# Tile 4's pair sums on GpSimd are held until tile 2's heads have been added on VectorE

## The reference, cut to what matters

```
x = x + L0_ffn(L0_cond(x, cond))          # attention, then product keys:
    sim = q . keys                        # per token, 8 heads, two halves of 32 keys
    all_scores = sx[..., :, None] + sy[..., None, :]
    scores, pk = top_k(all_scores, 8); h = gelu(x . down[idx])
    out = sum over heads and picks of softmax(scores) * h * up[idx]
x = x + L1_ffn(L1_cond(x, cond))          # 8 experts 128-256-256-128 (relu), top 2,
                                          # then 8 experts 128-512-128 (gelu), top 2
```

## Time and profile before

| | |
|---|---|
| median of 3 runs | 769.32 us (769.05 to 769.36) |
| the profiled execution | 770.8 us, of which 769.0 us span |
| PE busy | 730.4 us, 95% of the span |
| VectorE, ScalarE, GpSimd busy | 73%, 74%, 41% |
| mean granted TensorE clock | 0.991 of full |

### The profile page before, as it was taken

How to read it: one execution, slowest core, us unless ns; L and a number is a source line. 1 busy time by engine, 2 the same in 40 slices (tenths; PEclk the granted TensorE clock), 3 DMA queues, 4 the chain that set the end, 5 groups by cost and what they waited for, 6 DMA issues and landing times.

```text
span 769.0 us, 14737 instructions
## 1 busy us (share of the span) xinstructions
PE 730.4 (95%) x5250; PEld 644.6 (84%) x5250; DVE 560.2 (73%) x1495; ACT 572.4 (74%) x1001; POOL 312.3 (41%) x214
## 2 busy tenths in 40 slices
PE   6989998979768999999999999999999999999998
PEld 4767777879657898899899998988998999999887
DVE  3889997596699669777976897697779747834421
ACT  3788886299688789779868987897798689453243
POOL 2122221499993546175325635461753251000000
PEclk9999999989989999999999999999999999999999
DMA  8940000000000000000000000000000000000000
GB/s 312 339 128 2 3 1 2 1 1 1 1 0 1 1 2 7 1 2 7 1 3 0 9 1 2 1 8 0 2 8 0 2 1 8 1 1 9 1 1 7
DMA packets 11159, 16.91 MB, mean 22 GB/s; under 512 B 680, under 2 KB 6992, under 8 KB 10832
## 3 DMA queue, kind: packets, MB, share of 16 engines
q1 hardware_dynamic: 10944, 15.72, 6.3%
q10 hardware_dynamic: 144, 0.26, 0.1%
HBM read 14.93 MB, written 1.05 MB: 21 GB/s over the span
## 4 chain that ended last, share of the span: by engine, by line
PE 82%; DVE 8%; issue 5%; ACT 3%; DMA 1%; SPq 0%; DVEq 0%; ACTq 0%
PE banks L453 77%; PE banks L489 3%; DVE W_both L1223 2%; PE banks L703 2%; ACT G_both L947 2%; DVE W_both L1455 1%; DMA region<-in_pA 1%; ACT region L1024 1%; DVE acc L1601 1%; DVE HF L1461 0%; PE banks L735 0%; DVE region L1216 0%; ACT region L1030 0%; DVE PT L1553 0%; PE banks L796 0%
## 5 line engine op out<-in xcount | busy, mean ns | idle before, releaser
L395 POOL TENSOR_TENSOR region<-sim 128x1024 f32<-128x1024 f32 x128 | 261.6, 2072 | 95.8 <-DVE top_keys L1412 58.7
L1086 ACT ACTIVATE HF<-banks,lpack 128x256 f32<-128x256 f32 x256 | 105.4, 479 | 55.6 <-PE banks L453 54.6
L1024 ACT ACTIVATE region<-region,neg_thr 128x1024 f32<-128x1024 f32 x128 | 143.8, 1153 | 0.0
L1455 DVE SCALAR_TENSOR_TENSOR W_both<-region,rz_rel,W_both 128x1024 f32<-128x1024 f32 x98 | 139.9, 1428 | 2.0 <-DVE W_both L1455 0.5
L453 PE MATMUL banks<-HF,w_sb 128*128 128x256 f32 x512 | 123.2, 384 | 5.9 <-DVE HF L1461 5.8
L453 PEld LDWEIGHTS banks<-f_sb,HF 128*128 128x128 f32 x1024 | 123.7, 192 | 3.4
L1030 ACT ACTIVATE region<-region,dtop 128x1024 f32<-128x1024 f32 x114 | 125.4, 1142 | 0.0
L453 PE MATMUL banks<-f_sb,HF 128*128 128x128 f32 x1024 | 124.5, 275 | 0.0
L453 PE MATMUL banks<-cT,f_sb 128*128 128x256 f32 x512 | 122.7, 382 | 0.1
L453 PEld LDWEIGHTS banks<-HF,w_sb 128*128 128x128 f32 x512 | 94.6, 193 | 17.7 <-DVE HF L1461 6.7
L453 PEld LDWEIGHTS banks<-cT,f_sb 128*128 128x128 f32 x512 | 92.1, 190 | 16.3 <-issue 2.9
(11 more groups left out here) (167 smaller groups left out, 1011.5 us busy)
## 6 DMA issues: line engine op xcount, KB each, us to landing
w_sb<-in_w SPq DMA_DIRECT2D x1, 2048.0 KB, 12.8
f_sb<-in_f SPq DMA_DIRECT2D x1, 2048.0 KB, 15.5
region<-in_wq SPq DMA_DIRECT2D x1, 1024.0 KB, 8.6
region<-in_wqT SPq DMA_DIRECT2D x1, 1024.0 KB, 10.8
w_sb<-in_w SPq DMA_DIRECT2D x1, 1024.0 KB, 8.5
out_x<-acc_f SPq DMA_DIRECT2D x16, 64.0 KB, 1.6
x1T_all<-in_xT SPq DMA_DIRECT2D x1, 768.0 KB, 8.0
region<-in_pA SPq DMA_DIRECT2D x1, 588.5 KB, 6.5
```

The lines of the kernel that those rows point to most:

```text
L395: pool.tensor_tensor(S[a][h].rearrange("p (i j) -> p i j", i=NK), sim[t % 3][:, h, :].unsqueeze(2).broadcast_to([P, NK, NK]), sim[t % 3][: ...
L1024: act.activation(S[a][h], S[a][h], ACT.Prelu, bias=neg_thr[t % 4][:, h:h + 1], alpha=STEEP).then_inc(h_L, 1)
L1086: m = act.activation(HF[e % 2][:, f, :], bank(2 + b, 256 * (f % 2), 256 * (f % 2) + 256), ACT.Gelu_apprx_tanh, bias=L("bf", 4 * e + f, 4 * ...
L1455: v.scalar_tensor_tensor(W[a], S[a][h], rz_rel[a][:, h:h + 1], W[a], ALU.mult, ALU.add).then_inc(h_w, 1)
```

## The change

In turn 1, and only there, GpSimd waits ahead of tile 4's head 3 until h_w is 7, which is when all seven additions of tile 2 are done. Without it head h waits for h_w at h. Heads 4 to 7 stand behind head 3 in GpSimd's list and so are held as well, and so is the copy behind them. No instruction is added, removed or put in another place on any engine but the wait.

```
                 if more:
                     for h in range(8):
+                        if g == 1 and h == 3:
+                            pool.wait_ge(h_w, 7)
                         pair_scores(t + 2, 0, h)
                 keep_x2(t, 0)
```

## The result

Over six runs of each, the changed kernel takes 772.41 us (772.02 to 772.95) and the kernel before 769.54 (769.05 to 770.59): ratio 1.0034, 95% interval 1.0023 to 1.0045, 2.9 us slower. 772.2 had been predicted.

A forecast was written before the change was run, and what follows sets the result against it. VectorE was taken to bound turn 1 ahead of L796, and PE the stretch from there on. VectorE's net +1.24 us and the clock's 1.7 made +2.9, so 772.2 us, with an 8 in 10 range of 768.5 to 774.2.

The forecast's parts named there:

- What it takes away: VectorE from 225.2 us to tile 2's last addition runs undisturbed: 4.23 us saved, 3.08 left after waits for PE.
- What it adds: Tile 3's four additions on VectorE each meet one of GpSimd's held pair sums: 4.32 us of new loss.
- On PE: Small gaps in turn 1 gather into one of 3.7 us, from 245.65 to L796's start at 249.34.
- The net delay: VectorE's new loss less its saving, 4.32 - 3.08, delays the end by +1.24 us.
- The clock: PE's granted clock falls at the new gap; price 1.7 us, the middle between nothing and 3.4.
- The full loss of 2.8: By the skill's rule, each wait lowers PE's clock: 2.8 us on top of 1.24, in sum +4.0.
- The prediction's main ground for a clock that stays up: PE's clock stayed at 1.00 through the gap of 1.76 us ahead of turn 1.
- Clock up: Rival: PE's clock stays up behind the new gap, only +1.24 us remains, 770.6 us; chance 0.27.
- The third addition in between: Rival: tile 3's third addition on VectorE runs before the next pair sum, saving 1.87 us, 768.7 us; chance 0.11.
- The faster one: Rival: held sums cost VectorE nothing in tile 3; PE's three gaps, 2.69 us, are gained, 766.6 us; chance 0.10.

The follow-up runs named there:

- hold5: The changed kernel with the wait asking for h_w at 5 instead of 7; 769.97 us against 769.61 for the kernel before.
- hold9: The changed kernel with the wait asking for h_w at 9 instead of 7; 770.12 us against 769.61 for the kernel before.
- hold11: The changed kernel with the wait asking for h_w at 11 instead of 7; 770.88 us against 769.61 for the kernel before.
- fill: The changed kernel plus six unused 128x256 matmuls on PE in the gap ahead of L796; 770.73 us against 769.61 for the kernel before.
- hold11_fill: The changed kernel with the wait at 11 and five unused matmuls on PE ahead of the gate's matmuls; 769.79 us against 769.70 before.

## Why the prediction was right

**What it takes away: right.** L1447 fell to 0.23, the single addition to 1.28, the pair to 2.65. Tile 2's last addition ended at 233.54, 15.54 after the mark; 234.51 - 218.62 = 15.89 was predicted. The 0.35 is the wait for expert 6's values: 1.03 was forecast (230.07 - 229.07, the two times it comes from, is 1.00), 0.63 came. I had taken PE's group ahead of it from before with its 1.71 us; part of it ran at the lower clock, and this time it took 1.37, as the clock was back 10.4 us after the mark instead of 11.1. That is not the change: the clock's fall in the gap of 4.6 us, ahead of all that the change does, had come 0.7 us sooner too.

**What it adds: right.** From tile 2's last addition to the end of the eighth expert the prediction had 10.45 + 4.32 = 14.77 us; measured are 248.27 - 233.54 = 14.73. Each of the four additions met a sum, the third one too. hold5, hold9 and hold11 move the number of meetings, and L798 moves with it.

**On PE: right in kind.** One gap, of 3.30 us instead of 3.7, for the 0.35 above. The net delay was +0.85 instead of +1.24.

**The clock: right, and the price near by luck.** It fell, for 3.4 us and not for 6.8, and cost 1.55 where 1.7 was taken. The 1.7 was the middle between no fall and a fall of 6.8 us and not the price of what came. The full loss of 2.8, which the prediction drew from the Trainium skill ("TensorE: Matmul & The Clock Gate", section on HAM oscillation), did not come; the kernel of that section has waits of about 3 to 5 us, which the prediction left out. That the gap brings the fall about is shown by fill; that it falls in each run is not, as hold9's spread says. The sum in the traces is +2.40, in the medians +2.87; 0.5 us between them I can't place. So 772.2 is nearer to the measured 772.41 than its parts are to theirs: 1.24 + 1.7 stood for 0.85 + 1.55 and 0.5 whose cause stays open.

The prediction's main ground for a clock that stays up does not hold. It read from one trace that the clock stayed up behind the gap of 1.76. In the changed kernel, whose work up to there is the same, the clock fell near 201.1, behind the same gap:

```profile
199.24 0.33 PE L718 MATMUL banks<-ident,x2s 128*128 128x128 f32 x1 [1.77 <-DVE x2s L1473]
...
200.40 3.07 PE L455 MATMUL banks<-x2T,w_sb 128*128 128x256 f32 x8
```

```profile
202.00:203.00 1.00, 1.00 (x4) 0.81 (x3) 0.97 (x5) 1.00 (x2) 1.00 (x2) 0.50 0.00 0
```

It fell there in all nine traces of held kernels; the one before is the exception.

**The rivals.** Clock up: this is what fill shows, +1.12. The third addition in between: did not happen. The faster one was wrong in its price, not only in its mechanism: it gave 2.69 us, PE's three gaps, if the sums cost VectorE nothing. hold11 made that condition true and gained nothing, and with the clock up (hold11_fill) at most the half microsecond that ScalarE leaves. I had read what PE waits for up to L796 and not what the next group behind it needs. The rows could have told: ScalarE's copy for the gate came at 248.85 before, right behind its table load. (The wait of 0.5 us for cT in the earlier trace rows is another one, near 735 us.)

## What to carry to other kernels

Holding one engine back to free another moves their meetings to where it is let go, so count what the released work will run beside, and release it behind the last stretch that the bound depends on. Where small waits of the matrix engine gather into one, count the clock too. Here unused matmuls in the gap brought the key scores 1.4 to 1.7 us sooner in each of the three kernels that were run with and without them (gaps of 3.30, 2.03 and 2.03 us). Before pricing a gain by the waits that it removes, look up what the same engine's next group needs and when that is ready: here ScalarE's list left only half a microsecond.

## What the runs showed of the hardware that was not expected

The granted clock fell behind gaps of PE that were shorter than I had thought enough: 2.03 us in hold11, 1.27 and 0.53 in hold9, and 1.76 near 199 us in every trace but the one before, while 2.06 and 0.87 in hold5 left it up. It did so after PE had resumed, 0.6 us later in the changed kernel. So no length of a gap in these traces divides falls from none. And it differs from run to run: one kernel's executions spread over up to 4.6 us (hold9), the fastest at a mean clock of 0.991 and the four slowest at 0.984, against 1.9 for the kernel before.
